# Mixture-of-experts layer: the ScalarE/VectorE share of the activation roundings changed from 2:2 to 3:1

## The chip, the core and the metric

The kernel runs as one program on one core of a Trainium2 chip. The metric is the device time of one execution in microseconds (us), so lower is faster. Three timed runs before the change gave 1056.45, 1057.16 and 1059.05 us; their median is 1057.16 us. A NeuronCore has a matmul engine (TensorE, PE in the profile; its weight loads stand apart as PEld), VectorE (DVE), ScalarE (ACT), GpSimd (POOL) and SyncE (SP), which here only issues DMAs. They run on their own and wait for each other on semaphores.

## The reference

Two pre-norm transformer layers over 2,048 tokens of width 128, all in float32. Cut to what matters:

```python
x = x + _L0_attn_ref(_layernorm(x), ...)       # causal attention, 16 heads of 64
x = x + _L0_ffn_ref(_layernorm(x), ...)        # a linear layer with four low-rank experts
x = x + _L1_attn_ref(_layernorm(x), ...)       # attention by squared distance, 16 heads of 8
x = x + _L1_ffn_ref(_layernorm(x), ...)        # the mixture of experts, the part that changes

def _L1_ffn_ref(x, Wr1, br1, Wr2, br2, Ws1, bs1, Ws2, bs2, We1, be1, We2, be2):
    gates = jax.nn.softmax(jax.nn.relu(xf @ Wr1 + br1) @ Wr2 + br2, axis=-1)
    tg, ti = jax.lax.top_k(gates, 2)
    tg = jax.nn.softmax(tg / 2, axis=-1)
    out = jax.nn.silu(xf @ Ws1 + bs1) @ Ws2 + bs2            # the shared expert
    for e in range(8):                                       # 128 -> 512 -> 128
        h = jax.nn.silu(xf @ We1[e] + be1[e]) @ We2[e] + be2[e]
        out = out + jnp.sum(tg * (ti == e), axis=-1)[:, None] * h
    return out
```

## The kernel before, in words

The mixture of experts is the last part of the program, from about 836 us on. It goes over nine experts: the shared one (q = 0) and eight more, each computed for all tokens. An expert is worked in four **blocks** of 512 tokens (tb = 0 to 3), so there are 36 blocks; block k = 4q + tb. The loop that lays them out is `experts`, which each engine's program calls with its own functions.

To keep float32 accuracy, every factor is split into a rounded part ("high", in the type fp32r) and the rest ("low"), and a product is three matmuls: high by high, high by low, low by high.

- **PE** (`up_pe`, `down_pe`): the up-projection of a block is four groups of three matmuls (i = 0 to 3, one group for each 128 of the 512 inner columns), into PSUM banks 0, 1, 2, 0. The down-projection is four groups of three as well, all added into one bank; its group i needs the high part and the low part of inner columns i (L1701 to L1709). The order is up(k), down(k-1), up(k+1), down(k), and so on.
- **ACT** (`expert_act`): four SiLUs (L1729) from PSUM into `hid`, and the roundings of inner columns 0 and 1 (L1723), placed after the third and the fourth SiLU.
- **DVE** (`expert_dve`): the roundings of inner columns 2 and 3 (L1740) and the subtraction that gives the low part of column 3 (L1742). Behind it in the same block stands `evict_dve` for block k-1: bias and gate from PSUM (L1759), and the addition into the sum (L1762). In the second block of each expert (tb = 1) there follows `split_dve`: rounding (L1674) and low part (L1676) of the next expert's weights, 1,024 columns wide.
- **POOL** (`expert_pool`): the low parts of inner columns 0, 1 and 2 (L1773), in this order; columns 0 and 1 wait for ACT's roundings and column 2 for DVE's.

`hid` and `act2` (the high and low parts) have two halves that blocks use in turn. Each engine carries out its own instructions strictly in the order in which they are written: a waiting instruction holds up all behind it.

Of the kernel before, what the change touches and what calls it, by code (L numbers as in the profile page):

```python
# [48 lines left out]
NI = INNER // P  # L49
# [35 lines left out]
def build_kernel(nc, a, out, stop):  # L85
    ctx = ExitStack()
    with ctx:
# [3 lines left out]
        def sem(name):  # L91
            return ctx.enter_context(nc.semaphore(name))
# [94 lines left out]
        act2 = [flat(i).rearrange("p (b i s) -> p b i s", b=2, i=NI) for i in (1, 2)]  # L187
        hid = prob[:, 0:4, :].rearrange("p (b i) (k c) -> p b (i k) c", b=2, k=2)
# [41 lines left out]
        s_xs, s_ws, s_hhA, s_hhV, s_hlP, s_hlV, s_y = (sem(n) for n in (  # L230
            "x_split", "weights_split", "act_rounded01", "act_rounded23", "act_split012", "act_split3", "sums_turned"))
# [3 lines left out]
        s_rh, s_rhe, s_r1, s_lo, s_gc, s_ga, s_gT, s_gTe, s_oh, s_up, s_hid, s_down, s_xe = (sem(n) for n in (  # L235
            "router_hidden", "router_relu", "router_ones", "router_logits", "gate_chain", "gate_act", "gates_turned", "gates_stored",
            "first_marked", "up_done", "silu_done", "down_done", "expert_added"))
# [1456 lines left out]
        def down_pe(pe, q, w, tb, first):  # L1694
            k = 4 * q + tb
            if first:
                pe.wait_ge(s_rhe, 4)
            else:
                pe.wait_ge(s_yg, k - 3)
            for i in range(NI):  # L1700
                if i < 2:  # L1701
                    pe.wait_ge(s_hhA, 2 * k + i + 1)
                else:
                    pe.wait_ge(s_hhV, 2 * k + i - 1)
                if i < 3:
                    pe.wait_ge(s_hlP, 3 * k + i + 1)
                else:
                    pe.wait_ge(s_hlV, k + 1)
                wd = slice(INNER + i * P, INNER + (i + 1) * P)  # L1709
                for a_, b_ in ((0, 0), (0, 1), (1, 0)):  # L1710
                    mm = pe.matmul(banks[:, 4 + tb, :], w2[:, w, a_, wd], act2[b_][:, tb % 2, i, :],  # L1711
                                   start=(i == 0 and a_ == 0 and b_ == 0), stop=(i == NI - 1 and a_ == 1))
            mm.then_inc(s_down, 1)

        def expert_act(act, q, w, tb, first):
            k = 4 * q + tb
            early = first and tb < 2

            def rounded(i):
                act.wait_ge(s_hid, NI * k + i + 1)  # L1720
                if i == 0 and not early:
                    act.wait_ge(s_down, k - 1)
                act.activation(act2[0][:, tb % 2, i, :], hid[:, tb % 2, i, :], ACT.Copy).then_inc(s_hhA, 1)  # L1723
            for i in range(NI):
                act.wait_ge(s_up, NI * k + i + 1)
                if i == 0 and not early:
                    act.wait_ge(s_hlP, 3 * (k - 1))
                    act.wait_ge(s_hlV, k - 1)
                act.activation(hid[:, tb % 2, i, :], banks[:, i % 3, :], ACT.Silu, bias=w1[:, w, 2 * INNER + i:2 * INNER + i + 1]).then_inc(s_hid, 1)  # L1729
                if i >= 2:  # L1730
                    rounded(i - 2)

        def expert_dve(dve, q, w, tb, first):

            k = 4 * q + tb
            if not (first and tb < 2):
                dve.wait_ge(s_down, k - 1)
            for i in (2, 3):
                dve.wait_ge(s_hid, NI * k + i + 1)
                dve.tensor_copy(act2[0][:, tb % 2, i, :], hid[:, tb % 2, i, :]).then_inc(s_hhV, 1)  # L1740
            dve.wait_ge(s_hhV, 2 * k + 2)
            dve.tensor_tensor(act2[1][:, tb % 2, 3, :], hid[:, tb % 2, 3, :], act2[0][:, tb % 2, 3, :], ALU.subtract).then_inc(s_hlV, 1)  # L1742

        def evict_dve(dve, q, w, tb, first):
# [19 lines left out]
        def expert_pool(pool, q, w, tb, first):  # L1764
            k = 4 * q + tb
            if not (first and tb < 2):
                pool.wait_ge(s_down, k - 1)
            for i in range(3):
                if i < 2:
                    pool.wait_ge(s_hhA, 2 * k + i + 1)  # L1770
                else:
                    pool.wait_ge(s_hhV, 2 * k + 1)
                pool.tensor_tensor(act2[1][:, tb % 2, i, :], hid[:, tb % 2, i, :], act2[0][:, tb % 2, i, :], ALU.subtract).then_inc(s_hlP, 1)  # L1773

        def experts(e, head, tail=None, split=None, then={}, final=None):
# [109 lines left out]
        @block.scalar  # L1885
        def _(act):
            act.preload_act_table_set("natural_log_exp_and_others")
            ln_act(act, 0)

            act.wait_ge(s_cb, 1)  # L1890
            act.activation(cb[:, :], banks[0:HEADS, 4, 0:D], ACT.Copy, scale=SCALE0).then_inc(s_cbe, 1)
            attn0_act(act)
            attn1_act(act)
            ln_act(act, 1)
            gates_act(act)
            experts(act, expert_act, then={0: gate_exp_act, 1: gate_exp2_act})

        @block.vector
        def _(dve):
            dve.memset(ones[:, :], 1.0).then_inc(s_setup, 1)  # L1900
            dve.memset(msk[:, 0:BLK - P], 0.0).then_inc(s_setup, 1)
            dve.memset(hg[:, :, RSUM:RSUM + 1].rearrange("p n o -> p (n o)"), 0.0).then_inc(s_setup, 1)
            dve.memset(mx[:, :, :].rearrange("p k c -> p (k c)"), 0.0).then_inc(s_setup, 1)
            ln_dve(dve, 0, lambda e, n: e.wait_ge(s_x[n // 4], 16) if n % 4 == 0 else None)
            xsplit0_dve(dve)
            dve.wait_ge(s_const, 16)
            dve.tensor_copy(msk[:, BLK - P:BLK], cst[:, C_MS:C_MS + P]).then_inc(s_setup, 1)


            dve.wait_ge(s_cb, 2)  # L1910
            dve.wait_ge(ln[0]["norm"], NT - len(LN_ACT))
            dve.wait_ge(ln[0]["norm_act"], len(LN_ACT))
            for b in range(BATCH):
                for i in range(2):
                    xs = x[:, b * TB + 4 * i:b * TB + 4 * i + 4, :].rearrange("p t d -> p (t d)")
                    dve.tensor_tensor(xs, banks[:, 5 + i, :], xs, ALU.add).then_inc(s_cbe, 1)
            dve.wait_ge(s_cbe, 5)

            attn0_dve(dve)
            attn1_dve(dve)  # L1920
            ln_dve(dve, 1, lambda e, n: e.wait_ge(s_x1, 4) if n == 0 else None)
            xsplit_dve(dve)
            experts(dve, expert_dve, evict_dve, split_dve, then={0: gates_dve, 1: gates2_dve, 3: gates_out_dve}, final=final_dve)

        @block.tensor
        def _(pe):
            pe.wait_ge(s_const, 16)
            ln_pe(pe, 0)
            pe.wait_ge(ln[0]["xT"], 4)
            pe.wait_ge(s_setup, N_SETUP)  # L1930
            pe.wait_ge(s_wp, 48)
            for i in range(TB):
                mm = pe.matmul(banks[0:HEADS, 4, 0:D], bv2[:, :], wpr[:, i, :], start=(i == 0), stop=(i == TB - 1))
            mm.then_inc(s_cb, 1)
            pe.wait_ge(s_cbe, 1)
            for p in range(TB):
                mm = pe.matmul(banks[:, 5 + p // 4, (p % 4) * P:(p % 4 + 1) * P], pick[:, p, :], cb[:, :], start=True, stop=True)
            mm.then_inc(s_cb, 1)

            attn0_pe(pe)  # L1940
            attn1_pe(pe)
            ln_pe(pe, 1)
            router_pe(pe)
            experts(pe, up_pe, down_pe, then={0: logits_pe, 3: gates_pe}, final=final_pe)
# [55 lines left out]
```

## Time and profile before

| | |
|---|---|
| median of three timed runs | 1057.16 us |
| the profiled execution | 1059.26 us |
| its span, first to last instruction | 1057.5 us |
| PE busy | 995.2 us, 94% of the span |
| DVE busy | 716.7 us, 68% |
| ACT busy | 702.5 us, 66% |
| POOL busy | 555.1 us, 52% |

The busy shares are means over stages that differ much. The page's strip of 40 slices (26.4 us each) shows it; the experts fill the last eight. Each digit is the busy share in tenths.

```profile
PE   5779999999999999999999999999995699999997
DVE  5767777777778877778554433542213699999998
ACT  2346656665666665556578998899995566666663
POOL 3167777877777678767730000000000357887885
```

An engine's "idle before" is the time just ahead of its instructions in which it did nothing, with what ended it.

### The profile page before, as it was taken

What the parts mean: (1) busy time and instruction counts of PE and PEld (TensorE: products, weight loads), DVE (VectorE), ACT (ScalarE), POOL (GpSimd) and SP (SyncE); (2) the same over time, 40 slices, a digit from 0 to 9 for tenths busy, and PEclk for the clock granted to TensorE, in tenths of its full rate; (3) what the DMA queues carried; (4) which work ended last, traced back from release to release, by engine and by line L of the source; (5) the groups of instructions that cost most, each with busy time, mean ns of one, the idle gap of its engine ahead of it and who ended that gap; (6) DMA issues with size and microseconds to landing.
All of it is one profiled execution on the core that took longest, in us unless ns stands there. A gap on an engine that the chain in (4) does not pass through costs nothing.

```text
span 1057.5 us, 18841 instructions
## 1 busy us (share of the span) xinstructions
PE 995.2 (94%) x6927; PEld 589.5 (56%) x6927; DVE 716.7 (68%) x1480; ACT 702.5 (66%) x1023; POOL 555.1 (52%) x501
## 2 busy tenths in 40 slices
PE   5779999999999999999999999999995699999997
PEld 4446666666666566665543323323221577777775
DVE  5767777777778877778554433542213699999998
ACT  2346656665666665556578998899995566666663
POOL 3167777877777678767730000000000357887885
PEclk9899999999999999999999999999998699999999
DMA  3000000000000000100000000000000002211201
GB/s 97 8 8 2 9 9 8 9 9 9 8 1 9 9 9 8 23 39 1 3 3 8 12 10 11 10 12 10 11 9 11 1 8 115 100 60 61 78 40 40
DMA packets 24927, 23.52 MB, mean 22 GB/s; under 512 B 17612, under 2 KB 20316, under 8 KB 23820
## 3 DMA queue, kind: packets, MB, share of 16 engines
q1 hardware_dynamic: 24844, 22.42, 7.5%
q8 instruction: 52, 0.85, 0.3%
q14 instruction: 31, 0.25, 0.1%
HBM read 19.20 MB, written 1.11 MB: 19 GB/s over the span
## 4 chain that ended last, share of the span: by engine, by line
PE 66%; DVE 19%; issue 9%; ACT 4%; SPq 1%; DMA 1%; DVEq 0%; ACTq 0%
PE banks L481 11%; PE banks L1333 11%; PE banks L1319 6%; DVE big L1740 6%; PE banks L339 5%; PE banks L406 4%; PE banks L455 4%; PE banks L500 3%; PE banks L489 3%; PE banks L461 3%; PE banks L457 3%; PE banks L459 3%; PE banks L432 3%; ACT prob L605 2%; PE banks L1234 1%
## 5 line engine op out<-in xcount | busy, mean ns | idle before, releaser
L894 POOL TENSOR_TENSOR pacc<-pacc,prob 128x1024 f32<-128x1024 f32 (+3 forms) x157 | 267.9, 1706 | 65.1 <-ACT prob L605 52.8
L1346 ACT ACTIVATE prob<-banks 128x1024 f32<-128x1024 f32 x256 | 240.7, 1070 | 21.1 <-PE banks L1319 19.9
L605 ACT ACTIVATE prob<-banks 128x1024 f32<-128x1024 f32 (+1 forms) x160 | 150.4, 941 | 129.8 <-PE banks L461 124.9
L1773 POOL TENSOR_TENSOR big<-prob,big 128x512 fp32r<-128x512 f32 x108 | 164.6, 1544 | 60.5 <-ACT big L1723 33.9
L481 PE MATMUL banks<-prob,v 128*64 128x512 f32 (+3 forms) x768 | 142.9, 493 | 0.0
L1729 ACT ACTIVATE prob<-banks,w 128x512 f32<-128x512 f32 x144 | 94.5, 688 | 71.8 <-PE banks L1691 71.6
L1333 PE MATMUL banks<-prob,v 128*32 128x512 f32 x1024 | 136.2, 604 | 1.2 <-DVE pacc L1354 0.7
L1248 POOL TENSOR_TENSOR wqkv<-wqkv 64x512 f32<-64x512 f32 x8 | 8.3, 1034 | 196.1 <-DVE wqkv L1244 196.1
L1711 PE MATMUL banks<-big 128*128 128x512 f32 x432 | 106.9, 393 | 4.5 <-POOL big L1773 4.5
L1691 PE MATMUL banks<-big 128*128 128x512 f32 x432 | 107.3, 398 | 0.5 <-ACT prob L1729 0.5
L1319 PE MATMUL banks<-big 32*128 32x512 f32 x512 | 100.9, 503 | 0.8 <-ACT prob L1346 0.7
L883 POOL TENSOR_SCALAR_AFFINE_SELECT prob<-prob 128x256 f32<-128x256 f32 x128 | 51.7, 416 | 86.4 <-ACT prob L605 86.4
L1319 PEld LDWEIGHTS banks<-big 32*128 32x128 f32 x512 | 43.2, 181 | 94.7 <-ACT prob L1346 61.4
L1711 PEld LDWEIGHTS banks<-big 128*128 128x128 f32 x432 | 80.5, 188 | 25.0 <-POOL big L1773 5.6
L732 DVE TENSOR_REDUCE mxa<-banks 128x2 f32<-128x1024 f32 x64 | 77.0, 1223 | 24.0 <-PE banks L406 23.2
L1691 PEld LDWEIGHTS banks<-big 128*128 128x128 f32 x432 | 82.2, 192 | 19.5 <-ACT prob L1729 1.4
L737 DVE CUSTOM_DVE_ANT_0 banks<-banks,msk,mxa 128x128 f32<-128x128 f32 (+3 forms) x128 | 65.6, 557 | 38.5 <-PE banks L406 37.9
L737 DVE CUSTOM_DVE_ANT_0 banks<-banks,msk 128x256 f32<-128x256 f32 (+3 forms) x128 | 59.7, 520 | 33.8 <-PE banks L406 33.8
L481 PEld LDWEIGHTS banks<-prob,v 128*64 128x64 f32 x768 | 49.5, 137 | 54.9 <-issue 42.2
L406 PE MATMUL banks<-big 64*128 64x512 f32 (+3 forms) x384 | 70.4, 392 | 9.9 <-DVE big L716 4.0
L455 PE MATMUL banks<-big 64*128 64x512 f32 (+3 forms) x384 | 73.6, 379 | 0.0
L457 PE MATMUL banks<-big 64*128 64x512 f32 (+3 forms) x384 | 67.1, 345 | 0.0
(261 smaller groups left out, 1666.8 us busy)
## 6 DMA issues: line engine op xcount, KB each, us to landing
prob<-gate_rows SPq DMA_DIRECT2D x8, 1024.0 KB, 4.7
w<-in_experts SPq DMA_DIRECT2D x9, 514.0 KB, 3.6
wqkv<-in_wqkv SPq DMA_DIRECT2D x16, 193.0 KB, 2.4
x<-in_x SPq DMA_DIRECT2D x4, 256.0 KB, 4.1
zz<-pacc SPq DMA_DIRECT2D x64, 16.0 KB
wpr<-pacc SPq DMA_DIRECT2D x64, 16.0 KB
out<-x SPq DMA_DIRECT2D x4, 256.0 KB, 2.3
wpr<-in_wpr SPq DMA_DIRECT2D x1, 512.0 KB, 5.8
```

Of the source, the lines that this page charges most:

```text
L406: mm = pe.matmul(banks[:, bank + h, at:at + width(s, c)], qh[HP[h], w, s * P:(s + 1) * P], kh[HP[h], w, c * BLK:c * BLK + width(s, c)], st ...
L455: pe.matmul(banks[:, bank + h, at:at + wd], kh[HP[h], w, k], qh[HP[h], w, q], start=True, stop=False)
L481: mm = pe.matmul(banks[HP[h], 4 + half, o:BLK], v[:, w, t, HP[h]], pr[:, g % NRING, h, at:at + wd], start=(t == 0), stop=(t == (2, 7)[half]))
L605: act.activation(pr[:, g % NRING, :, 0:wd], banks[:, 2 * (j % 2):2 * (j % 2) + 2, 0:wd], ACT.Exp, scale=SCALE0).then_inc(s_exp, 1)
L737: ins = dve.tensor_tensor_reduce(out=sc, in0=sc, in1=msk[:, BLK - wd:BLK], scale=1.0, scalar=low, op0=ALU.add, op1=ALU.max, accum_out=mx[: ...
L894: pool.tensor_tensor(pacc[:, half, :, o:BLK], pacc[:, half, :, o:BLK], p_[:, :, at:at + wd], ALU.add).then_inc(s_padd, 1)
L1319: mm = pe.matmul(banks[:, 2 * pair1(n) + k, :], l1[hr, w, t * P:(t + 1) * P], r1[hr, w, sbk * BLK:(sbk + 1) * BLK], start=True, stop=True)
L1333: mm = pe.matmul(banks[32 * h:32 * h + 32, 6, :], qv[:, u % 2, t, h, :], prob[:, prob1(2 * m + h // 2), h % 2 * BLK:(h % 2 + 1) * BLK], st ...
L1346: act.activation(prob[:, prob1(n), :], banks[:, 2 * pair1(n):2 * pair1(n) + 2, :].rearrange("p b c -> p (b c)"), ACT.Exp, scale=2 * SCALE1 ...
L1691: mm = pe.matmul(banks[:, i % 3, :], w2[:, w, a_, i * P:(i + 1) * P], x2[:, b_, c], start=(j == 0), stop=(j == 2))
L1711: mm = pe.matmul(banks[:, 4 + tb, :], w2[:, w, a_, wd], act2[b_][:, tb % 2, i, :], start=(i == 0 and a_ == 0 and b_ == 0), stop=(i == NI - ...
L1773: pool.tensor_tensor(act2[1][:, tb % 2, i, :], hid[:, tb % 2, i, :], act2[0][:, tb % 2, i, :], ALU.subtract).then_inc(s_hlP, 1)
```

## The change

The rounding of inner column 2 goes from DVE to ACT, behind ACT's two others. The semaphore counts follow: ACT's count goes up by three in a block, DVE's by one, and POOL's subtraction of column 2 now waits for ACT.

```diff
@@ down_pe
             for i in range(NI):
-                if i < 2:
-                    pe.wait_ge(s_hhA, 2 * k + i + 1)
+                if i < 3:
+                    pe.wait_ge(s_hhA, 3 * k + i + 1)
                 else:
-                    pe.wait_ge(s_hhV, 2 * k + i - 1)
+                    pe.wait_ge(s_hhV, k + 1)
@@ expert_act
                 if i >= 2:
                     rounded(i - 2)
+            rounded(2)
@@ expert_dve
-            for i in (2, 3):
-                dve.wait_ge(s_hid, NI * k + i + 1)
-                dve.tensor_copy(act2[0][:, tb % 2, i, :], hid[:, tb % 2, i, :]).then_inc(s_hhV, 1)
-            dve.wait_ge(s_hhV, 2 * k + 2)
+            dve.wait_ge(s_hid, NI * k + 4)
+            dve.tensor_copy(act2[0][:, tb % 2, 3, :], hid[:, tb % 2, 3, :]).then_inc(s_hhV, 1)
+            dve.wait_ge(s_hhV, k + 1)
             dve.tensor_tensor(act2[1][:, tb % 2, 3, :], hid[:, tb % 2, 3, :], act2[0][:, tb % 2, 3, :], ALU.subtract).then_inc(s_hlV, 1)
@@ expert_pool
             for i in range(3):
-                if i < 2:
-                    pool.wait_ge(s_hhA, 2 * k + i + 1)
-                else:
-                    pool.wait_ge(s_hhV, 2 * k + 1)
+                pool.wait_ge(s_hhA, 3 * k + i + 1)
                 pool.tensor_tensor(act2[1][:, tb % 2, i, :], hid[:, tb % 2, i, :], act2[0][:, tb % 2, i, :], ALU.subtract).then_inc(s_hlP, 1)
```

On DVE, from the weights' split in the second block of expert 1 to the end of that expert (each block: rounding, subtraction, eviction, addition; `big` holds the high and low parts, `prob` the SiLU outputs, `pacc` the sum):

```order
 L1674 CAST big<-w 128x1024
 L1676 TENSOR_TENSOR big<-w,big 128x1024
-L1740 CAST big<-prob 128x512 x2
+L1740 CAST big<-prob 128x512
 L1742 TENSOR_TENSOR big<-prob,big 128x512
 L1759 SCALAR_TENSOR_TENSOR zero<-banks,b2T,prob 128x512
 L1762 TENSOR_TENSOR pacc<-pacc,zero 128x512
-L1740 CAST big<-prob 128x512 x2
+L1740 CAST big<-prob 128x512
 L1742 TENSOR_TENSOR big<-prob,big 128x512
```

Each block has one rounding where there were two; nothing else moves on this engine. On POOL, the subtractions of the first two blocks of the experts, with the semaphores they wait for (`act_rounded01` is counted up by ACT, `act_rounded23` by DVE); first before, then after:

```order
-L1773 TENSOR_TENSOR big<-prob,big 128x512 [waits act_rounded01] x2
-L1773 TENSOR_TENSOR big<-prob,big 128x512 [waits act_rounded23]
-L1773 TENSOR_TENSOR big<-prob,big 128x512 [waits act_rounded01] x2
-L1773 TENSOR_TENSOR big<-prob,big 128x512 [waits act_rounded23]
```
```order
+L1770 TENSOR_TENSOR big<-prob,big 128x512 [waits act_rounded01] x6
```

POOL's order is the same, and none of its instructions waits for DVE's roundings any more.

## Rows read from the trace of the kernel before

**Rows 1.** Busy time of each engine: blocks 4 to 31, and one expert (q = 4).
```profile
core 0: us, PE busy (x) PEld busy (x) DVE busy (x) ACT busy (x) POOL busy (x), PEclk, DMA share, GB/s
865.73:1024.20 158.47, 154.70 (x673) 125.50 (x672) 156.31 (x155) 99.30 (x168) 127.34 (x83) 1.00 0.22 77
933.82:956.44 22.62, 22.10 (x98) 17.94 (x96) 22.31 (x23) 14.07 (x24) 18.64 (x13) 1.00 0.21 70
```
**Rows 2.** PE in order of time: start us, us, what, idle before and its releaser.
```profile
944.76 2.88 PE L1691 MATMUL banks<-big 128*128 128x512 f32 x12
947.48 2.88 PE L1711 MATMUL banks<-big 128*128 128x512 f32 x12
950.20 2.88 PE L1691 MATMUL banks<-big 128*128 128x512 f32 x12
952.92 1.52 PE L1711 MATMUL banks<-big 128*128 128x512 f32 x6
954.96 1.64 PE L1711 MATMUL banks<-big 128*128 128x512 f32 x6 [0.52 <-POOL big L1773]
956.44 2.88 PE L1691 MATMUL banks<-big 128*128 128x512 f32 x12
```
**Rows 3.** Waits from 880 to 1034 us: total us, times, longest.
```profile
POOL big L1773 <- DVE big L1740: 22.9, 27, 2.2
PE banks L1711 <- POOL big L1773: 3.8, 7, 0.7
```
**Rows 4.** DVE in order of time, around the weights' split of the second block.
```profile
927.42 1.78 DVE L1674 CAST big<-w 128x1024 fp32r<-128x1024 f32 x1
929.23 1.23 DVE L1676 TENSOR_TENSOR big<-w,big 128x1024 fp32r<-128x1024 f32 x1
930.37 0.76 DVE L1740 CAST big<-prob 128x512 fp32r<-128x512 f32 x2
931.16 1.66 DVE L1742 TENSOR_TENSOR big<-prob,big 128x512 fp32r<-128x512 f32 x1
```
**Rows 5.** POOL in the same stretch.
```profile
926.90 1.74 POOL L1773 TENSOR_TENSOR big<-prob,big 128x512 fp32r<-128x512 f32 x1
930.87 3.11 POOL L1773 TENSOR_TENSOR big<-prob,big 128x512 fp32r<-128x512 f32 x2 [2.23 <-DVE big L1740]
```
**Rows 6.** POOL and DVE in order of time, an ordinary block.
```profile
918.87 1.66 DVE L1742 TENSOR_TENSOR big<-prob,big 128x512 fp32r<-128x512 f32 x1
920.46 0.74 DVE L1759 SCALAR_TENSOR_TENSOR zero<-banks,b2T,prob 128x512 f32<-128x512 f32 x1
921.23 1.02 DVE L1762 TENSOR_TENSOR pacc<-pacc,zero 128x512 f32<-128x512 f32 x1
922.17 1.51 DVE L1740 CAST big<-prob 128x512 fp32r<-128x512 f32 x1
...
918.58 1.41 POOL L1773 TENSOR_TENSOR big<-prob,big 128x512 fp32r<-128x512 f32 x1 [0.36 <-DVE big L1740]
920.21 3.18 POOL L1773 TENSOR_TENSOR big<-prob,big 128x512 fp32r<-128x512 f32 x2 [0.22 <-ACT big L1723]
...
925.65 1.30 POOL L1773 TENSOR_TENSOR big<-prob,big 128x512 fp32r<-128x512 f32 x1 [0.49 <-ACT big L1723]
```
**Rows 7.** Groups by line, 780 to 1057 us: DVE beside an idle POOL.
```profile
L1617 DVE TENSOR_TENSOR big<-xT,big 128x512 fp32r<-128x512 f32 x4 | 2.8, 692 | 0.1
L1615 DVE CAST big<-xT 128x512 fp32r<-128x512 f32 x4 | 1.7, 421 | 0.0
```
**Rows 8.** ACT in order of time, one block (its up-projection starts at 922.12).
```profile
924.95 0.62 ACT L1723 ACTIVATE big<-prob 128x512 fp32r<-128x512 f32 x1
925.47 0.68 ACT L1729 ACTIVATE prob<-banks,w 128x512 f32<-128x512 f32 x1
926.04 0.63 ACT L1723 ACTIVATE big<-prob 128x512 fp32r<-128x512 f32 x1
928.58 1.92 ACT L1729 ACTIVATE prob<-banks,w 128x512 f32<-128x512 f32 x3 [1.90 <-PE banks L1691]
```
**Rows 9.** DVE and ACT in blocks 4 and 5, before the first split of the loop.
```profile
869.08 0.68 ACT L1729 ACTIVATE prob<-banks,w 128x512 f32<-128x512 f32 x1
869.41 2.95 DVE L1740 CAST big<-prob 128x512 fp32r<-128x512 f32 x2
874.52 0.68 ACT L1729 ACTIVATE prob<-banks,w 128x512 f32<-128x512 f32 x1
875.10 2.94 DVE L1740 CAST big<-prob 128x512 fp32r<-128x512 f32 x2
```
**Rows 10.** The end of the program in order of time.
```profile
1048.28 1.66 DVE L1742 TENSOR_TENSOR big<-prob,big 128x512 fp32r<-128x512 f32 x1
1049.53 1.62 PE L1711 MATMUL banks<-big 128*128 128x512 f32 x6 [0.50 <-POOL big L1773]
1051.24 0.68 DVE L1811 TENSOR_TENSOR x<-banks,x 128x512 f32<-128x512 f32 x1
1051.84 0.74 DVE L1759 SCALAR_TENSOR_TENSOR zero<-banks,b2T,prob 128x512 f32<-128x512 f32 x1
```

## The prediction

> **What bounds the kernel now.** I read the busy strip by stage first: only the last eight slices contain the changed code, and there PE and DVE both show nines. The table by stretch sharpens it: over blocks 4 to 31 DVE is busy 156.31 of 158.47 us and PE 154.70 [rows 1]. PE in order of time tells which of the two limits. An up- or down-projection takes 2.72 us from start to start (944.76, 947.48, 950.20), so a block costs 5.44 us and an expert 21.76. The traced expert takes 22.62 [rows 1]. The missing 0.87 us is one stall: a down-projection stops after six matmuls until POOL's third subtraction is done [rows 2]. There are seven such waits, one per expert in the loop [rows 3]. From 865.73 to 1024.20 are 28 blocks, 152.32 us of matmuls, so the stalls sum to 6.15 us: that is all that the change can win in the loop.
>
> The list of waits says who is behind it: POOL's third subtraction waits for DVE's rounding 27 times, 22.9 us in all [rows 3]. In the block of the weights' split DVE works through 1.78 + 1.23 us of weights first, the two roundings end only at 931.13, and POOL, idle for 2.23 us, starts at 930.87 as the first is done [rows 4, 5]. PE waits for that POOL operation. The change takes exactly this chain away.
>
> **Why a busy DVE is not simply relieved: the turns.** DVE's busy time is mostly waiting. Its subtraction takes 0.69 us beside an idle POOL [rows 7] and 1.66 us in the loop; the rounding 0.42 [rows 7] and 1.51 [rows 6]. The starts and ends show a strict rule. POOL's operation at 918.58 ends at 919.99, DVE's subtraction issued at 918.87 ends at 920.53, so its 0.69 us ran from 919.84, 0.15 before POOL's end. The other way round: DVE's addition ends at 922.25, POOL's next operation ends at 923.39, and its own time is 1.30 us [rows 6], so it ran from 922.09, 0.16 before. One operation at a time, first come first served. In **turns** (own time less 0.15, and 0.14 for POOL) this costs: POOL's subtraction 1.16, DVE's rounding 0.27, subtraction or addition 0.54, the weights' rounding 0.55 (issued at 927.42 behind a POOL operation that ends at 928.64, ended at 929.20: 0.70 own), the weights' subtraction 1.08 (its 1.23 was measured while POOL was idle) [rows 4, 5]. The eviction reads PSUM and stays at 0.74 whatever POOL does.
>
> The page "SBUF — State Buffer", section "SBUF: two separate sides", of the Trainium skill calls the shared port pair an exclusive lock held for the whole instruction, so that the loser fully blocks. The trace agrees but for the last 0.15 us. By the page's letter every turn would be 0.15 longer, DVE would be later by about 1 us at each stall below, and the sum would be some 3 us higher.
>
> **The change part by part.** *ACT* gets 36 roundings of 0.63 us. In a block it is idle 1.90 us before its first SiLU [rows 8]; 0.52 of additional start-to-start time leave 1.3 idle. Nothing queues behind it late. Cost 0, and if the cover were gone, 0.5 per block. The third rounding ends 0.52 after the second, at 5.1 us after the start of the up-projection (926.67 + 0.52 - 922.12). *POOL*'s third subtraction can start then, at once behind its second. *The stall of 0.87 us* therefore goes in all seven experts: -6.15 us.
>
> What is late next is **DVE's subtraction for column 3**. Let T be the start of a block's up-projection. The first rounding lets POOL start at T+3.53 (925.65 less 922.12) [rows 6, 8]. The fourth group of this block's down-projection starts at T+10.20 (three projections and three groups of 0.68). POOL no longer pauses for DVE, so every DVE operation queues behind one of POOL's. Two steady states come out of the turns.
>
> *DVE ahead*: rounding and subtraction sit behind POOL's first and second; the subtraction ends at 3.53 + 1.16 + 0.27 + 1.16 + 0.69 = T+6.81, 3.4 us early. *DVE behind*: the order is POOL 1, addition of the former block, POOL 2, rounding, POOL 3, subtraction: 3.53 + 3 x 1.16 + 0.54 + 0.27 + 0.69 = T+8.51, 1.7 us early. From POOL 1 to the issue of the next addition are 3 x 1.16 + 2 x 0.54 + 0.27 = 4.83 in turns, then +0.15 - 0.08 + 0.74 + 0.03 for the end of the subtraction and the eviction: 5.67 us. The next POOL 1 comes after 5.44, so it is first by 0.23 us and DVE stays behind: it does not use its freed 0.4 us to catch up.
>
> *The weights' split, met ahead*: rounding issued at T+8.43, free at 8.98; POOL 1 of the next block until 10.14; weights' subtraction until 11.22; POOL 2 until 12.38; rounding; POOL 3 until 13.81; subtraction ends at 14.50 against a need at 10.20 + 5.44 = 15.64. No stall, and DVE is behind from there. *Met behind*: POOL 1 and addition until 5.23, POOL 2 until 6.39, weights' rounding 6.94, POOL 3 8.10, weights' subtraction 9.18, POOL 1 10.34, rounding 10.61, POOL 2 11.77, subtraction ends at T+12.46 against 10.20: a stall of 2.26, with 0.1 to reach PE 2.35 us. During it POOL runs out of input, and DVE is ahead again. So the stalls come in every second expert. In blocks 4 and 5 DVE's rounding starts right as the fourth SiLU ends [rows 9] (2.94 us are two roundings behind two POOL operations), so it is ahead when the first of the seven splits comes: absorbed, stall, absorbed, stall, absorbed, stall, absorbed. Three stalls: +7.05 us. The weights' subtraction behind a running POOL is not in this trace; it lies between 1.23 and 1.23 + 1.16, and I take what the order of turns gives, 1.0 of wait. With none, the stall is 1.3 us and three make 4; with all, 2.5 and 7.5.
>
> *The end*: the last eviction is issued at 1051.84 behind DVE's lag, though its matmuls ended at 1051.15 [rows 10]. One rounding less ahead of the subtraction of 1048.28 lets it start about 0.2 after the matmuls: -0.5 us (between 0 and -0.5; POOL's three subtractions still hold the matmuls before it).
>
> Sum against the profiled execution's 1059.26: -6.15 + 7.05 - 0.5 = +0.4, so 1059.7. The median of the runs lies 2.1 below the profiled time; on it the forecast is 1057.16 + 0.4 = **1057.6 us**.
>
> **Rivals.**
> *A, the relief arrives.* If DVE recovers the lead, all splits are absorbed and no stall is left: -6.15 - 0.5, 1050.5 us. It hangs on the 0.23 us by which POOL's first operation beats the addition; turns 0.04 shorter each (there are six) would do it. Against it: the turns are read to 0.02. For it: the whole sum of 5.67 is a new pattern. The Trainium skill's page "Perfetto Trace Analysis", section "Optimizing Scalar/DVE Operations", says that where DVE is saturated, offloading to Scalar may make sense; DVE at 156 of 158 us is such a case, and by that rule A would be the outcome.
> *B, a stall in every expert.* Met ahead, the split is absorbed with 14.50 against 15.64. If the chain there is over 1.14 us longer (one more POOL turn of 1.16 before it), or if DVE does not get ahead in a stall, all seven experts lose 2.35: 16.45 - 6.15 - 0.5 = +9.8, 1067.0 us.
> *C, the old stall stays in size.* DVE's last subtraction takes the place of POOL's third with the same 0.87: only the end gains, 1056.7 us. It would be so if POOL's turns did not push DVE in the split; the turns of [rows 6] speak against it.
>
> **How the numbers follow.** A change under 0.3%, 3.2 us, can't be told from none here. Forecast 0.58, with 1056 to 1060.5 as its own range (four stalls instead of three, if the first split meets DVE behind, give +2.75, which lies at its edge: 0.04 of it counts as slower); A 0.22, faster; B 0.09, slower; C 0.11, same. Faster 0.22, same 0.54 + 0.11 = 0.65, slower 0.13. The range takes in A and leaves out B: 1050.3 to 1061.0.
>
> **What would show it.** Right: no PE wait for POOL's subtraction in the loop, but three waits of 2.2 to 2.5 us for DVE's L1742, each before a fourth group of a third block; experts of 21.8 and 24.1 us in turn; the weights' subtraction at about 2.2 us instead of 1.23; DVE's addition at 1.6 in the blocks behind a split; POOL's wait for DVE's rounding gone and its own 108 operations no slower than 1.85; ACT's idle time before its first SiLU down to 1.3. Wrong: experts of 21.8 throughout (A), of 24 throughout (B), of 22.6 (C).

## The result, and the profile after

The change made the kernel slower: 1063.78 us median of five runs (1063.19 to 1065.44) against 1057.16 (1054.91 to 1059.67), a ratio of 1.0064 with a 95% interval of 1.0044 to 1.0084. The forecast was 1057.6 us, and the range ended at 1061.0. In the profiled executions the time from block 4 to block 32 rises from 158.47 to 164.48 us, +6.01, and the rest behind it falls from 33.29 to 32.58, -0.71. The medians rise by 6.6 us, and by the interval the rise is 4.7 to 8.9, so the sum of +5.3 lies inside it. (What lies ahead of block 4 differs by 1.3 us between the two executions, in code that is the same.)

Three stretches of the profile after, each one expert long, give the busy time of each engine and, near the line's end under PEclk, the granted clock of TensorE as a share of its 2.4 GHz.

```profile
core 0: us, PE busy (x) PEld busy (x) DVE busy (x) ACT busy (x) POOL busy (x), PEclk, DMA share, GB/s
864.39:886.15 21.76, 21.76 (x98) 18.02 (x97) 18.95 (x20) 16.75 (x28) 15.86 (x12) 1.00 0.35 127
886.15:910.90 24.75, 22.56 (x98) 18.36 (x96) 24.44 (x18) 16.19 (x28) 20.67 (x14) 0.98 0.24 84
910.90:933.73 22.83, 22.83 (x97) 18.79 (x96) 19.06 (x20) 16.36 (x28) 15.76 (x11) 0.95 0.16 50
```

Against the even 22.62 of [rows 1], experts now alternate: 21.76, 24.75, 22.83, 24.59, 23.00, 24.41, 23.14 us. The forecast had the alternation, but with 21.76 for every short one. The third line shows the surprise: this expert has no stall, PE is busy in all 22.83 us, and it is still 1.07 longer than its eight projections at 2.72 make it. The clock is at 0.95.

Two lines from the list of waits of the profile after, from 864 to 1029 us (total us, times, longest), answer [rows 3].

```profile
POOL big L1770 <- ACT big L1723: 39.4, 28, 4.9
PE banks L1711 <- DVE big L1742: 6.6, 3, 2.2
```

Seven waits for POOL have become three for DVE's subtraction. PE in order of time around the first of them, the counterpart of [rows 2]:

```profile
902.47 2.88 PE L1691 MATMUL banks<-big 128*128 128x512 f32 x12
905.19 2.20 PE L1711 MATMUL banks<-big 128*128 128x512 f32 x9
909.57 1.53 PE L1711 MATMUL banks<-big 128*128 128x512 f32 x3 [2.19 <-DVE big L1742]
910.90 3.94 PE L1691 MATMUL banks<-big 128*128 128x512 f32 x12
914.68 2.89 PE L1711 MATMUL banks<-big 128*128 128x512 f32 x12
```

The wait stands before the fourth group of the third block's down-projection, as forecast, and the gap in the work is 2.34 us, from 907.23, when a tenth matmul would have started, to 909.57 (2.35 at the two later stalls). But the next up-projection takes 3.94 us instead of 2.88, and starts 0.65 late after its three down matmuls. Busy time and clock of the same stretch:

```profile
902.47:910.90 8.43, 6.24 (x26) 4.84 (x24) 8.33 (x6) 4.05 (x7) 7.33 (x5) 0.93 0.21 64
910.00:912.00 2.00, 2.00 (x6) 1.58 (x5) 1.93 (x4) 0.00 (x0) 0.56 (x1) 0.50 0.03 8
910.90:914.30 3.40, 3.40 (x12) 2.72 (x11) 2.60 (x5) 1.49 (x3) 0.00 (x0) 0.68 0.00 0
914.30:930.00 15.70, 15.70 (x71) 12.99 (x70) 12.80 (x11) 11.51 (x21) 12.49 (x9) 1.00 0.19 67
```

The granted clock is 0.68 on the mean of this up-projection, a mixture of 1.2 and 2.4 GHz, and 1.00 again behind it. Before the fall PE had worked without a pause until 907.4 and then idled 2.19 us. The record of the clock shows three such falls to 0.5 in the loop, of 3.41 us each, from 909.67, 957.45 and 1005.24, one behind each stall; the kernel before has none there. The Trainium skill describes this on the page "TensorE: Matmul & The Clock Gate", section "HAM oscillation — how this bites in real kernels": a wait between stretches of matmuls makes the next stretch start at the half clock. The trace agrees on that. The waits of the page's kernel are for DMA and 3 to 5 us long; here 2.19 us of waiting for DVE were enough. The prediction gave the clock no term.

DVE and POOL in order of time, around the same split, answer [rows 4, 5]:

```profile
900.79 1.61 DVE L1762 TENSOR_TENSOR pacc<-pacc,rall 128x512 f32<-128x512 f32 x1
902.32 1.77 DVE L1674 CAST big<-w 128x1024 fp32r<-128x1024 f32 x1
904.12 2.20 DVE L1676 TENSOR_TENSOR big<-w,big 128x1024 fp32r<-128x1024 f32 x1
906.24 1.52 DVE L1740 CAST big<-prob 128x512 fp32r<-128x512 f32 x1
907.79 1.63 DVE L1742 TENSOR_TENSOR big<-prob,big 128x512 fp32r<-128x512 f32 x1
...
900.55 4.68 POOL L1770 TENSOR_TENSOR big<-prob,big 128x512 fp32r<-128x512 f32 x3 [1.01 <-ACT big L1723]
905.99 4.57 POOL L1770 TENSOR_TENSOR big<-prob,big 128x512 fp32r<-128x512 f32 x3 [0.76 <-ACT big L1723]
```

This is the chain of turns as it was worked out. The addition is issued 0.24 us behind POOL's first operation (900.79 and 900.55; worked out: 0.23) and takes 1.61 us. The weights' subtraction, 1.23 us when POOL stood idle in [rows 4], takes 2.20. The up-projection of the block whose rounding stands behind the split (the third of the expert) starts at 897.03, and the subtraction for its column 3 ends at 909.42, 12.39 us later; the turns gave 12.46.

### The profile page after: what moved, and what is told of

Same layout as the page of the kernel before. It is cut to its first block, busy times and chain, and to the rows that moved or that the text cites. A ratio compares the mean times of both kernels' runs of the same rounds, so it can differ in the third digit from the quotient of the medians.

```text
span 1061.4 us, 18868 instructions
## 1 busy us (share of the span) xinstructions
PE 996.0 (94%) x6927; PEld 591.2 (56%) x6927; DVE 708.7 (67%) x1444; ACT 720.8 (68%) x1059; POOL 554.1 (52%) x501
## 4 chain that ended last, share of the span: by engine, by line
PE 74%; DVE 12%; issue 6%; ACT 4%; SPq 1%; DMA 1%; POOL 0%; DVEq 0%; POOLq 0%; ACTq 0%
PE banks L481 11%; PE banks L1333 10%; PE banks L1319 6%; PE banks L339 5%; PE banks L1691 4%; PE banks L406 4%; PE banks L1711 4%; PE banks L455 4%; PE banks L500 3%; PE banks L489 3%; PE banks L461 3%; PE banks L459 3%; PE banks L457 3%; PE banks L432 3%; DVE big L1740 2%
## 5 line engine op out<-in xcount | busy, mean ns | idle before, releaser
L1711 PE MATMUL banks<-big 128*128 128x512 f32 x432 | 107.0, 395 | 7.3 <-DVE big L1742 6.6
L1691 PE MATMUL banks<-big 128*128 128x512 f32 x432 | 110.9, 407 | 0.6 <-ACT prob L1729 0.6
L1691 PEld LDWEIGHTS banks<-big 128*128 128x128 f32 x432 | 85.4, 199 | 20.8 <-ACT prob L1729 1.5
L1711 PEld LDWEIGHTS banks<-big 128*128 128x128 f32 x432 | 81.4, 190 | 26.2 <-issue 9.5
```

The lines of the kernel that those rows point to most:

```text
L1691: mm = pe.matmul(banks[:, i % 3, :], w2[:, w, a_, i * P:(i + 1) * P], x2[:, b_, c], start=(j == 0), stop=(j == 2))
```

## The experiments

Two theories stood against each other after the result: that each stall costs its 2.35 us and a fall of the clock behind it, and that the stalls themselves cost more than worked out. Beside that, the older claim was open that DVE is in one of two states, and not just busy. The kernel before was timed again beside the experiments, with medians of 1058.24 (17 runs) and 1058.46 us (24 runs); the ratios below are to these runs.

**Keep the clock up.** PE gets matmuls that nobody uses to fill its wait; results are unchanged.

```diff
             for i in range(NI):
+                if i == 3 and tb == 2 and w == 0 and not isinstance(q, int):
+                    for _ in range(10):
+                        pe.matmul(banks[:, 3, :], w2[:, w, 0, 0:P], x2[:, 0, 0:BLK], start=True, stop=True)
```

> The changed kernel, with ten extra matmuls of 512 columns into an unused PSUM bank ahead of the fourth down group of the third block in experts 2, 4 and 6, where the trace after shows PE idle for 2.19 us and the granted clock then at 0.5 for 3.41 us. Theory (the three long stalls stay, and the clock that falls behind each of them costs the rest): ten matmuls at 0.227 us fill 2.27 us of each 2.35 us stall, the clock stays at 1.00, experts of 24.1 instead of 24.4 to 24.8 us, and the experts behind them 21.8 instead of 22.8 to 23.1; 3 x 1.7 = 5.1 us less than the changed kernel, about 1058.7 us. Rival (the excess has nothing to do with the clock and comes from the stalls' own queues): experts stay at 24.6 and 23.0, time 1063.8 or above.

Measured 1058.84 us, ratio to the kernel before 1.0010 (0.9995 to 1.0025). Busy time and clock of the whole loop in this kernel, and PE in order of time at the first stall:

```profile
865.00:1030.00 165.00, 165.00 (x726) 135.85 (x725) 154.71 (x132) 116.46 (x201) 129.50 (x86) 1.00 0.21 74
```
```profile
907.63 2.20 PE L1714 MATMUL banks<-big 128*128 128x512 f32 x9
909.67 2.43 PE L1703 MATMUL banks<-big 128*128 128x512 f32 x10
912.04 0.94 PE L1714 MATMUL banks<-big 128*128 128x512 f32 x3
912.82 2.91 PE L1691 MATMUL banks<-big 128*128 128x512 f32 x12
```

The ten matmuls (L1703) take the place of the wait, the clock holds at 1.00 and the next up-projection takes 2.91 us. Experts last 21.76, 24.23, 21.79, 24.22, 21.79, 24.23, 21.79 us. From block 4 to block 32 it is 159.81 us: 7.49 above the 152.32 of bare matmuls, so 2.5 for each of three stalls, and 4.67 below the changed kernel, so 1.56 for each fall of the clock. The gap itself is 2.37 us here (909.67 to 912.04). The first theory is shown; the second falls.

**Fill half of the wait.** The same with `range(5)`.

> As the kernel with ten fill matmuls, but with five: PE works 1.13 us of each 2.35 us stall and then idles about 1.2 us. The stall of 0.87 us in the kernel before did not lower the granted clock, the one of 2.35 us did. Theory 1 (it is the idle stretch that counts, and 1.2 us is nearer to 0.87): clock stays at 1.00, about 1059 us, experts of 24.2 and 21.8. Theory 2 (any stall above the old one lowers it): three falls again, 1063.8 us.

Measured 1058.90 us, ratio 1.0005 (0.9988 to 1.0023), and no fall of the clock in the loop; blocks 4 to 32 take 159.74 us. PE in order of time:

```profile
909.21 1.29 PE L1703 MATMUL banks<-big 128*128 128x512 f32 x5
911.58 0.93 PE L1714 MATMUL banks<-big 128*128 128x512 f32 x3 [1.07 <-DVE big L1745]
912.35 2.91 PE L1691 MATMUL banks<-big 128*128 128x512 f32 x12
```

An idle stretch of 1.07 us costs nothing beyond itself, one of 2.19 costs 1.56 more. Theory 1 holds: the third block is as late as before (the fourth group starts 2.37 us after the ninth matmul's turn ends), so it is not its lateness but PE's idleness that brings the clock down. Whether the unbroken length counts, or the sum of idle time, or when it falls, these runs don't separate: the five matmuls changed all three. The result also fits the kernel before, whose seven waits of up to 0.7 us [rows 3] left the clock at 1.00 [rows 1].

**Two states or a load?** The eviction is made narrower, by more and by less than the 0.24 us on which DVE's state hangs. Both kernels leave out the rest of each block's output.

```diff
-            dve.scalar_tensor_tensor(out=tmp[:, :], in0=banks[:, 4 + tb, :], scalar=bias, in1=gb[:, w, c],
+            c = slice(tb * BLK, tb * BLK + BLK // 2)
+            dve.scalar_tensor_tensor(out=tmp[:, 0:BLK // 2], in0=banks[:, 4 + tb, 0:BLK // 2], scalar=bias, in1=gb[:, w, c],
```

> The changed kernel, where the eviction with bias and gate (L1759) covers 256 of its 512 columns; the other half of each block's expert output is left out. It reads PSUM, so it takes no turn with POOL. Theory (DVE stays behind because the addition is issued 0.23 us after POOL's first operation): the eviction gets 0.27 shorter, the addition is issued 0.04 before POOL's, DVE gets ahead and stays there, all seven splits are absorbed, experts of 21.8 us, about 1051.5 us. Rival (DVE simply has too much work): 4 x 0.27 = 1.1 us less per expert takes about 1.1 from each stall of 2.35, three stalls of 1.3 remain, about 1057.

Measured 1052.25 us, ratio 0.9947 (0.9931 to 0.9964). All seven experts last 21.76 us. The block in which the order flips, DVE and then POOL in order of time:

```profile
897.11 0.47 DVE L1760 SCALAR_TENSOR_TENSOR zero<-banks,b2T,prob 128x256 f32<-128x256 f32 x1
897.62 0.69 DVE L1763 TENSOR_TENSOR pacc<-pacc,zero 128x512 f32<-128x512 f32 x1
...
897.66 4.93 POOL L1771 TENSOR_TENSOR big<-prob,big 128x512 fp32r<-128x512 f32 x3 [1.03 <-ACT big L1723]
```

The addition is issued 0.04 us ahead of POOL, as expected, and takes 0.69 us. One block earlier it was issued 0.03 us behind POOL (892.25 and 892.22) and took 1.81. And the other width, 416 columns:

> The changed kernel with the eviction 416 columns wide instead of 512 (the other 96 columns of each block's expert output are left out): 0.10 us shorter, less than the 0.24 us by which the trace after shows the addition (900.79) issued behind POOL's first operation (900.55). Theory (two states with a threshold): DVE stays behind, three stalls of 2.35 us with their clock falls, 1063.8 us, while 0.27 us less took all stalls away. Rival (a load effect, growing with each tenth): 0.10 of 0.27, so some 37% of the gain of 12, about 1059.5.

Measured 1062.86 us, ratio 1.0049 (1.0032 to 1.0066). DVE and POOL in order of time:

```profile
894.99 0.64 DVE L1760 SCALAR_TENSOR_TENSOR zero<-banks,b2T,prob 128x416 f32<-128x416 f32 x1
895.67 1.72 DVE L1763 TENSOR_TENSOR pacc<-pacc,zero 128x512 f32<-128x512 f32 x1
...
895.54 4.42 POOL L1771 TENSOR_TENSOR big<-prob,big 128x512 fp32r<-128x512 f32 x3 [1.02 <-ACT big L1723]
```

Now the addition comes 0.13 behind POOL and waits. All three stalls and all three falls of the clock are there; blocks 4 to 32 take 164.58 us, against 164.48 with the full width. Taking 0.10 us per block away gains nothing in the loop, taking 0.27 away gains all 12.16. The load rival falls in both. The threshold can also be read directly: from POOL's first operation to the next addition it is 5.68 us in the changed kernel (895.11 to 900.79), 5.57 with 416 columns (890.10 to 895.67) and 5.40 with 256 (892.22 to 897.62), and blocks come every 5.44; only the last is shorter, and only there DVE gets ahead.

**Spread the clump.** Same work, the weights' subtraction one block later.

```diff
-        def split_dve(dve, q, w):
+        def split_dve(dve, q, w, tb):
+            if tb == 1:
                 dve.wait_ge(s_ew[w], 8 * (q - w) + 16)
 ...
                 dve.tensor_copy(w2[:, w, 0, :], w1[:, w, 0:2 * INNER]).then_inc(s_ws, 1)
+                return
             dve.wait_ge(s_ws, 2 * q + 1)
 ...
-                    if split and tb == 1 and not last:
-                        split(e, q + 1, 1 - w)
+                    if split and tb in (1, 2) and not last:
+                        split(e, q + 1, 1 - w, tb)
```

> The changed kernel, where the weights' low part (the subtraction, 1024 columns) is taken in the third block of an expert instead of directly behind the weights' rounding in the second; the work is the same. Theory (the stall is the clump of both weight operations, each with a POOL turn ahead, on a DVE that is behind): each alone is absorbed, by the turns met ahead, no stall, experts of 21.8 us, about 1051.5 us. Rival (DVE's total is too much for PE's pace): stalls of the same sum, split over two blocks, 1060 or above.

Measured 1050.61 us, ratio 0.9945 (0.9928 to 0.9962). DVE in order of time over the two blocks:

```profile
902.14 0.68 DVE L1674 CAST big<-w 128x1024 fp32r<-128x1024 f32 x1
903.21 1.06 DVE L1741 CAST big<-prob 128x512 fp32r<-128x512 f32 x1 [0.39 <-ACT prob L1730]
...
907.59 1.21 DVE L1677 TENSOR_TENSOR big<-w,big 128x1024 fp32r<-128x1024 f32 x1
908.73 1.52 DVE L1741 CAST big<-prob 128x512 fp32r<-128x512 f32 x1
```

DVE meets both weight operations ahead: 0.68 and 1.21 us, where the clump took 1.77 and 2.20. After the first it even waits 0.39 us for ACT. All experts last 21.76 us.

**Let ACT round the weights**, on the changed kernel and on the kernel before. DVE's `split_dve` keeps its last wait and the subtraction.

```diff
+        def split_act(act, q, w):
+            act.wait_ge(s_ew[w], 8 * (q - w) + 16)
+            if not isinstance(q, int) or q > 1:
+                act.wait_ge(s_down, 4 * (q - 1))
+            act.activation(w2[:, w, 0, :], w1[:, w, 0:2 * INNER], ACT.Copy).then_inc(s_ws, 1)
```

> The changed kernel, where ACT also rounds the next expert's weights (1024 columns, some 1.05 us by its 0.62 for 512), in its 1.39 us of idle time before the first SiLU of the third block; DVE keeps the weights' subtraction. Theory: DVE loses one POOL turn and 0.70 us from the clump, 1.7 to 1.9 us, so met behind the stall is 0.6 at most, and in the steady pattern DVE gets ahead: no stall, experts of 21.8 us, about 1051.5 us. Rival (ACT becomes late: 4.8 + 1.05 us in a block of 5.44): up-projection waits for the SiLUs by 0.3 to 0.5 us per expert, 1055.

Measured 1050.59 us, ratio 0.9940 (0.9921 to 0.9958). No expert has a stall, and ACT is not late.

> The kernel before (two roundings each), where ACT rounds the next expert's weights (1.05 us by its 0.62 for 512 columns) and DVE keeps only their subtraction. Theory: DVE's chain ahead of POOL's third subtraction in the split's block gets 1.8 us shorter, more than the stall of 0.87 us, so the stall goes and PE's pace rules: experts of 21.8 us, about 1051.5 us, as good as the same edit on the changed kernel. Rival (with two roundings DVE's total still exceeds PE's pace and a stall comes back in a later expert): experts of 22.2 or more, 1054 or above.

Measured 1053.63 us, ratio 0.9958 (0.9943 to 0.9973). The stall of 0.87 is gone, but 0.10 to 0.13 us per expert remain in five experts, and one stall of 1.36 in the first, where ACT waits 2.5 us for the DMA of the weights. Two of the waits of this kernel, from 870 to 1030 us:

```profile
POOL big L1774 <- DVE big L1741: 14.0, 23, 1.5
ACT big L1673 <- DMA w<-in_experts: 2.5, 1, 2.5
```

These experts of 21.86 to 21.89 us lie between what the theory (21.8) and the rival (22.2 or more) gave, nearer to the theory. The median of 1053.63 does not: it lies near the rival's 1054, 2.1 above the theory's 1051.5. The profiled execution, at 1050.94 us, was the fastest of the seven, so where the others lose the rest is not shown. In the profiles the 28 blocks take 154.24 us here and 152.32 with the changed kernel, and 1.36 of these 1.92 us are the wait for the DMA. Whether the change under study is worth having once the clump is gone is therefore open: the two intervals overlap.

**All four roundings on ACT.** `rounded(3)` behind `rounded(2)`, and DVE waits for ACT's count of four before its subtraction.

> All four activation roundings on ACT, none on DVE. ACT then works 4 x 0.69 + 4 x 0.57 = 5.0 us of a 5.44 us block. Theory (turns): with one turn of 0.27 and one POOL turn of 1.16 less per block DVE gets ahead, no stall, experts of 21.8 us, about 1050.5 us. Rival (ACT becomes the bound or late with its fourth rounding, 0.5 us after the third): experts above 22 us, 1055 or more.

Measured 1051.24 us, ratio 0.9935 (0.9916 to 0.9954), experts of 21.76 to 21.86 us. ACT is on the edge (from 870 to 1030 us it waits only 14.9 us for PE, where in the changed kernel it waited 47.8 from 864 to 1029), but it does not become the bound.

## Why the prediction was wrong

- *The old stall goes, -6.15 us.* Right: no wait for POOL's third subtraction in the loop, and in the kernels without any stall the 28 blocks take the 152.32 us that the sum assumed.
- *ACT's third rounding costs nothing.* Right: its idle time ahead of the first SiLU went from 1.90 to 1.39 us (forecast 1.3), and no wait of PE for ACT stands in the loop. From the timeline of the profile after:

```profile
903.48 1.92 ACT L1729 ACTIVATE prob<-banks,w 128x512 f32<-128x512 f32 x3 [1.39 <-PE banks L1691]
```

- *DVE's turns behind POOL's, two states, stalls in every second expert, the first one absorbed.* Right in all its places. The narrower evictions put the threshold between 0.10 and 0.27 us, with the forecast 0.23 inside.
- *Three stalls, +7.05 us.* This is the step that failed: a term of the sum was too small. It priced a stall by its own length. The length was right, 2.35 us in the trace, and 7.49 for the three with the clock held up, but each of them also cost a fall of TensorE's clock, to which the sum gave nothing: 1.56 us, 4.67 in all. The term measured 12.16 us, not 7.05. The trace of before could have warned: its clock is 1.00 throughout the loop with waits of at most 0.7 us, and no row showed it to survive a wait three times as long.
- *The end, -0.5 us.* Measured -0.71, for the reason given: the last eviction is issued at 1055.78, 0.05 us behind the end of its matmuls (0.69 in [rows 10]).
- *The rivals.* A did not come, by the 0.24 us; the experiments that cross this threshold measure 1052.3, near its 1050.5. B and C did not come. The rival that was missing was the forecast itself with the clock's price, 1057.6 + 5.1.

With +0.4 of the working replaced by -6.15 + 12.16 - 0.71, the sum is +5.3, so 1062.5 on the earlier median; measured 1063.78. The missing 1.3 us lies within the measurement's uncertainty: against 1058.46 us, the median of the 24 later runs of the kernel before, the rise is 5.3 us.

## What to carry to other kernels

Where two engines take turns at a resource, moving work from one of them removes its wait for the other as well: here it let POOL run on without a pause, and DVE's remaining operations waited longer. Work out who is issued first in each turn, because a few hundredths of a microsecond can decide between two steady states. Price a wait of the matmul engine by its length and by what its clock does afterwards, and prefer several short waits to a long one (here seven with at most 0.7 us of idle time cost 6.15 us, three with 2.19 cost 12.16); large operations off the regular beat (here the next weights' split) are better spread over blocks than issued together: on top of the change that alone leads from 1063.78 to 1050.61 us, 0.55% below the kernel before, with no work removed.

## What the runs showed of the hardware

- TensorE's granted clock stayed at 1.00 across idle stretches of 0.7 and 1.07 us and fell to 0.5 for 3.41 us behind those of 2.19 us, in nearly the same loop. Ten or five unused matmuls in each gap prevented it, for a gain of 4.9 us over three gaps.
- In this loop VectorE's and GpSimd's operations on SBUF took turns in the order of issue. An addition issued 0.04 us ahead of POOL took 0.69 us; issued 0.03, 0.13 and 0.24 us behind it, it took 1.81, 1.72 and 1.61.
